# Masking one of six causal score tiles in VectorE's maximum instruction instead of by TensorE matmuls

## The reference, cut to what matters

```
causal_bias = where(i[None, :] <= i[:, None], 0.0, NEG)
for l in range(4):
    h = rmsnorm(x, n1[l])
    q, k, v = split(h @ Wqkv[l].T + bqkv[l], 3)
    q, k = apply_rope(q), apply_rope(k)
    s = einsum('bhqd,bhkd->bhqk', q, k) * scale + causal_bias
    x = x + (softmax(s) @ v merged over heads) @ Wo[l].T + bo[l]
    ... cross attention to the context, then a gated feed-forward block
```

## Time and profile before

| | us |
|---|---|
| median of 3 runs | 2112.79 (2111.06 to 2121.15) |
| time of the profiled execution | 2108.02 |
| its span, first to last instruction | 2106.3 |
| TensorE busy | 1821.6 (86%) |
| VectorE busy | 1414.7 (67%) |
| ScalarE busy | 1067.3 (51%) |
| GpSimd busy | 785.3 (37%) |

### The profile page before, as it was taken

One profiled execution on the slowest core, in us unless ns is written; L12 is line 12 of the kernel. 1 busy time (PEld: TensorE's weight loads), 2 busy tenths in 40 slices (PEclk: granted clock), 3 DMA queues, 4 the chain that ended last, 5 costly groups with the idle time before them and its releaser, 6 DMA issues. The chain is left out here.

```text
span 2106.3 us, 34605 instructions
## 1 busy us (share of the span) xinstructions
PE 1821.6 (86%) x12966; PEld 1123.3 (53%) x12971; DVE 1414.7 (67%) x3427; ACT 1067.3 (51%) x1523; POOL 785.3 (37%) x1131
## 2 busy tenths in 40 slices
PE   5978998584787898899899899999989999989978
PEld 4556665363454444565544464644555554456557
DVE  8667676552776877875577874577786466787475
ACT  2655655121453465564466566366656446656510
POOL 4423334403613554431455341255443154533130
PEclk9999998587787899999999999999999999999989
DMA  7443343121000000132000033000014000004200
GB/s 226 112 135 101 103 108 94 52 77 43 23 1 13 1 1 13 32 101 56 16 1 1 1 95 81 28 1 2 1 53 117 7 16 2 1 24 101 52 1 21
DMA packets 69995, 100.91 MB, mean 48 GB/s; under 512 B 17126, under 2 KB 35438, under 8 KB 69188
## 3 DMA queue, kind: packets, MB, share of 16 engines
q1 hardware_dynamic: 60612, 90.01, 14.9%
q0 software_dynamic: 9216, 8.69, 1.6%
HBM read 52.43 MB, written 12.38 MB: 31 GB/s over the span
## 5 line engine op out<-in xcount | busy, mean ns | idle before, releaser
L1778 DVE TENSOR_REDUCE maxima<-wide 128x2 f32<-128x512 f32 (+3 forms) x512 | 405.9, 818 | 133.7 <-PE wide L831 130.3
L2014 ACT ACTIVATE prob<-wide 128x768 f32<-128x768 f32 (+1 forms) x384 | 332.1, 881 | 146.0 <-PE wide L831 145.9
L1937 ACT ACTIVATE prob<-wide 77x1024 f32<-77x1024 f32 x256 | 257.8, 1017 | 91.9 <-PE wide L831 87.5
L831 PE MATMUL wide<-q_g 32*128 32x256 f32 (+3 forms) x2048 | 266.1, 390 | 38.2 <-ACT prob L2014 18.1
L2256 POOL TENSOR_SCALAR_AFFINE_SELECT prob<-prob 128x256 f32<-128x256 f32 (+1 forms) x384 | 184.8, 487 | 292.6 <-ACT prob L2014 291.0
L1454 DVE TENSOR_REDUCE maxima<-wide 128x8 f32<-128x616 f32 x256 | 202.8, 795 | 115.0 <-PE wide L831 109.4
L831 PEld LDWEIGHTS wide<-q_g 32*128 32x128 f32 x2048 | 138.4, 186 | 203.7 <-issue 99.8
L2078 POOL TENSOR_TENSOR rstd<-moments,cst 128x4 f32<-128x4 f32 x88 | 90.4, 1027 | 364.2 <-DVE moments L1342 171.5
L1858 ACT ACTIVATE q_g<-wide 128x1024 fp32r<-128x1024 f32 x128 | 131.1, 1024 | 185.0 <-PE wide L831 185.0
L831 PE MATMUL wide<-kx,q_g 128*128 128x312 f32 x512 | 180.7, 418 | 8.3 <-DVE maxima L1454 5.8
L2163 POOL DMA_DIRECT2D masked_k<-kx x224 | 121.3, 546 | 178.2 <-PE wide L831 177.0
(11 more groups left out here) (249 smaller groups left out, 3087.2 us busy)
## 6 DMA issues: line engine op xcount, KB each, us to landing
masked_q<-q_g SPq DMA_DIRECT2D x448, 64.0 KB
masked_q<-mask_l SPq DMA_DIRECT2D x84, 308.0 KB
masked_k<-kx POOLq DMA_DIRECT2D x224, 19.5 KB, 1.9
A<-in_w SPq DMA_DIRECT2D x2, 2048.0 KB, 11.9
unit_w<-in_unit_w SPq DMA_DIRECT2D x8, 448.0 KB, 3.8
ffn_w<-in_ffn_w SPq DMA_DIRECT2D x4, 768.0 KB, 4.7
slots_in<-v_third SPq DMA_DIRECT2D x1, 2560.0 KB, 12.4
prob<-slots_in SPq DMA_DIRECT2D x8, 320.0 KB, 3.3
```

What stands on the lines that cost most here:

```text
L831: return e.matmul(out, lhsT, rhs, start=start, stop=stop, is_transpose=turn)
L1778: e.tensor_reduce(top[:, t, h], v[:, :, at0:at0 + P * t + P], AX.X, ALU.max, negate=True).then_inc(*made("max", *([("free", tile)] if t == ...
L1937: e.activation(p[0:SC, :], s[0:SC, :], ACT.Exp, bias=0.0, scale=1.0).then_inc(*made("exp", pb, ("free", tile)))
L2014: e.activation(pv, sv, ACT.Exp, bias=0.0, scale=8 ** -0.5).then_inc(*made("exp", pb, ("free", tile)))
```

## The change

For the third tile (k = 2, `UNMASKED`) TensorE no longer adds the mask: its two matmuls with `causal_b` are left out, and the last score matmul of the tile is the one that VectorE waits for. In place of two `tensor_reduce` VectorE issues four `tensor_tensor_reduce`, one for each head and block: in0 is the scores in PSUM, in1 the mask as bf16 in SBUF, the sum is written back over the scores, and its largest value goes to `top`, one value per partition. To serve blocks of 128 and 384 columns alike, the constant is now a row of 384 zeros and the 128 columns of the mask, in bf16; a block of n columns takes the last n. It stands in `cst` as 256 words instead of 128. The maxima are no longer negated in any tile; instead the two rows of `k_tok` hold -1.0.

```
-for _n, _w in (("ident", P), ("causal", P), ...
+for _n, _w in (("ident", P), ("causal", S // 2), ...
+UNMASKED = 2
+        causal = const("causal").bitcast(BF)
 # TensorE, causal_max
-                        mm(s[:, at1:at1 + P * t + P], qk[r, 0, P * t:P * t + P], qk[r, 1, 0:P * t + P],
-                           start=t == blocks[0], stop=False)
+                        i_mm = mm(s[:, at1:at1 + P * t + P], qk[r, 0, P * t:P * t + P], qk[r, 1, 0:P * t + P],
+                                  start=t == blocks[0], stop=k == UNMASKED and t == blocks[-1])
-                for c in range(2):
+                for c in range(2 if k != UNMASKED else 0):
 # VectorE, begin
-            e.tensor_copy(causal_b[:, :], const("causal")).then_inc(*made("begin"))
+            e.tensor_copy(causal_b[:, :], causal[:, S - P:S]).then_inc(*made("begin"))
 # VectorE, causal_max
                 for t in blocks:
-                    e.tensor_reduce(top[:, t, h], v[:, :, at0:at0 + P * t + P], AX.X, ALU.max, negate=True).then_inc(
-                        *made("max", *([("free", tile)] if t == blocks[-1] else [])))
-                    at0 += P * t + P
+                    n, ends = P * t + P, [("free", tile)] if t == blocks[-1] else []
+                    if k == UNMASKED:
+                        for c, i in enumerate(heads_in):
+                            part = s[:, S * c + at0:S * c + at0 + n]
+                            e.tensor_tensor_reduce(part, part, causal[:, S - n:S], 1.0, NEG, ALU.add, ALU.max,
+                                                   top[:, t, i:i + 1]).then_inc(*made("max", *(ends if c == 1 else [])))
+                    else:
+                        e.tensor_reduce(top[:, t, h], v[:, :, at0:at0 + n], AX.X, ALU.max).then_inc(*made("max", *ends))
+                    at0 += n
 # GpSimd, clear
-                e.memset(k_tok[:, :, :, MROW:MROW + 2], 1.0).then_inc(*made("clear"))
+                e.memset(k_tok[:, :, :, MROW:MROW + 2], -1.0).then_inc(*made("clear"))
 # constants
-    put("causal", np.where(r[None, :] > r[:, None], NEG, 0.0))
+    late = np.concatenate([np.zeros((P, S - P)), np.where(r[None, :] > r[:, None], NEG, 0.0)], 1).astype(np.float32)
+    put("causal", (late.view(np.uint32) >> 16).astype(np.uint16).view(np.float32))
```

More of the change, by code:

```diff
@@ L37 @@
 _at = 0
-for _n, _w in (("ident", P), ("causal", P), ("cumul", P), ("cos", NI * 8), ("sin", NI * 8),
+for _n, _w in (("ident", P), ("causal", S // 2), ("cumul", P), ("cos", NI * 8), ("sin", NI * 8),
                ("kscale8", 1), ("kscale4", 1), ("pick", 2), ("position", NI), ("iota", SC), ("rev", E8), ("minus_half", NI),
@@ L156 @@
     tensor_reduce = tensor_copy = memset = reciprocal = bn_stats = bn_aggr = affine_select = dma_start = anything
-    indirect_dma_start = anything
+    indirect_dma_start = tensor_tensor_reduce = anything
 def interleaved(items):
```

## The result

The changed kernel took 2121.42 us (median of 11 runs) beside 2111.06 for the kernel before (11 runs, same chip): ratio 1.0058, 95% interval 1.004 to 1.0077. The medians are 10.4 us apart and the ratio makes 12 us, where 12 had been forecast. The profiled execution has a span of 2116.7 us, against 2106.3.

The account below looks back on a forecast made before the run. TensorE's order was taken to set the pace. VectorE's later return of the third tile summed to 13.8 us, less some 2 for short waits: 12 us on the 2112.79 median made 2124.8 us, range 2109 to 2150.

Parts of the forecast that it names:

- TensorE's saving is worth nearly nothing: Ahead of the fourth score tile: 20 us of removed matmuls only lengthen the wait for ScalarE, from 0.28 to 0.60 us.
- Rival 4: Ahead of the fourth tile: the wait shrinks in 48 groups by 0.32 us each, 15 us, giving 2097; chance 0.04.
- D = 1.80 us: VectorE's work on the third tile: four combined instructions take 1.80 us against 1.29 for the two reductions.
- rival 1: VectorE's third tile: the value beside the output is free, work 1.50 us, about +1 us, giving 2114; chance 0.28.
- four times 0.074 for the value beside the output: VectorE's third tile: each of the four instructions pays 0.074 us for its one value per partition, on top of 1.50.
- The starts: VectorE begins the third tile 0.32 us earlier where it was idle, not where it comes straight from other work.
- the turn waits for VectorE in nearly every group: TensorE's qk_turn for the next group waits for VectorE to return the third tile, by 0.12 to 0.42 us.
- the 25 groups: Commonest kind of head group: the next group's turn comes 0.19 us later in each, 4.8 us in all.
- the 8: Groups where VectorE comes straight from the key and query cut, without earlier start: 0.42 us each, 3.4 us.
- the 4: Groups where the turn already waits 0.50 us for VectorE: the end moves 0.19 us each, 0.8 us in all.
- The 11 groups: Second kind of head group: the turn at 1455.96 instead of 1455.84, 0.12 us each, 1.3 us in all.
- rival 3: VectorE's third tile: writing into PSUM in place halves the rate, work 2.88 us, about +70 us, 2183; chance 0.09.

Follow-up runs that it names:

- e1: Changed kernel, but TensorE also keeps its two mask matmuls on the third tile, so it is masked twice: 2123.43 us, ratio 1.0056 to before.
- e2: Changed kernel with no mask at all on the third tile, VectorE using plain reductions: 2103.93 us, ratio 0.9965 to before.
- e12: Changed kernel with the filler of e9 plus 20 matmuls of 256 zero columns inside the idle time in layer 0: 2107.02 us, ratio 1.000.
- e10: Kernel before (TensorE masks all six tiles, only the maxima's sign as in the changed kernel) with the filler of e9: 2095.13 us, ratio 0.9962.
- e3: Changed kernel with two matmuls of 256 zero columns added to one logits tile of every group: 2112.71 us, ratio 1.001 to before.
- e9: Changed kernel with matmuls of 384 zero columns in four groups: five in the second of layers 1 to 3, three in the sixth of layer 0; ratio 1.0026.
- e11: Changed kernel with no mask in any of the six maximum tiles, VectorE using plain reductions: 2088.27 us, ratio 0.993 to before.

## Why the prediction was right, and where it was not

The time came out 3.4 us below the forecast, and for a sum of which only about half was the right term. The kernel before, measured again, came out 1.7 us below the median that the forecast started from.

- *TensorE's saving is worth nearly nothing.* Right, and the row is the wait ahead of the fourth tile: 1.07, 1.08, 1.08 and 1.08 us after the exponential in before, changed, e1 and e2. Forecast for it was a wait of 0.60 us, measured 0.75, because the two matmuls held TensorE for 0.47 us and not for 0.32; with the wait behind them this cost nothing. Rival 4 (faster) fell on this row. e2 shows the limit of "nearly nothing": 0.07 us in the common groups, but 0.3 in fourteen others, some 5 us of the 20.
- *D = 1.80 us.* Mis-sized: 1.64 (median of the groups 1.635), halfway between it and rival 1's 1.50. The step that was mis-sized is "four times 0.074 for the value beside the output". The instructions follow one another every 0.49, 0.51 and 0.25 us, and three of the four accumulator reads run beside the next main instruction. What counts is one read of 0.14 us at the end: 1.50 + 0.14 = 1.64. The Trainium skill, "VectorE: DVE Perf Modes", section "Two Vector instructions with no wait between them", is borne out in that such an operation is two instructions; the price that I had put on the second one was my own, from the trains of bn_aggr in the earlier trace rows, and its place was wrong.
- *The starts.* Right: VectorE begins 0.32 us earlier relative to the exponential (0.09 us after it instead of 0.41), and where it comes straight from other work, as in the earlier trace rows, it doesn't. The counterpart of that row in the changed kernel:

```profile
1481.90 0.73 DVE L1274 TENSOR_SCALAR hid<-rope_b 128x512 int32<-128x512 int32 x1 [0.81 <-POOL rope_b L2240]
...
1482.56 0.55 DVE L1788 CUSTOM_DVE_ANT_0 wide<-wide,cst 128x384 f32<-128x384 f32 x1
...
1484.24 0.66 PE L836 MATMUL wide<-cst,hid 128*128 128x128 f32 x4
```

  The turn starts 1.68 us after the custom instruction, 1.43 in the earlier trace rows; these 8 groups lost 0.30 us each. The sign that the turn waits for VectorE in nearly every group, came in about half: in 35 of the 64 the turn's weight load waits for it, by 0.16 us in the common groups and 0.36 in those of the earlier trace rows; in groups such as the one shown after the result it does not.
- *The terms by kinds.* With D = 1.64 each forecast falls by 0.16 us: 0.03 (measured 0.02) for the 25 groups, 0.26 (0.30) for the 8, 0.03 (0.02) for the 4, and 0.35 for the second to fourth of layer 0. There the two filled kernels (e12 and e10), whose time at the low clock in these groups is the same, differ by 0.30, 0.17 and 0.35. Two terms were wrong for their own sake. The 11 groups lost 0.07 where -0.04 would follow (VectorE starts only 0.27 us earlier in them; the rest is not accounted for), and the first groups of the layers nothing instead of 0.15. In the latter the third tile's reductions start 1.19 us after the group's first reduction instead of 1.48, so 0.29 us earlier and not the 0.20 of idleness in the earlier trace rows that I had allowed. The last groups of the layers lost 0.23 each, 0.9 together, forecast 1.0. Layer 0 lost 1.3 us and layer 1 1.1 between the filled kernels; with layers 2 and 3 taken as layer 1 and the last groups added, that makes 5.5 us for the mechanism for which 12 had been forecast. The quiet groups give 5.6 and 6.1 with the last groups added.
- *The rival that was missing.* No rival had the clock in it. I had read 1.00 in the two windows of the earlier trace rows and argued from steady stretches, where it is 1.00 after the change as well. The profile of before held the sign: 79 us at the lower level between 640 and 1890 us, most of them in the first groups of layers, where TensorE waits for other engines. At one place, the sixth group of layer 0, the changed kernel lost 3.5 us by it in both profiles and the kernel before nothing. In the second groups of layers 1 to 3 the clock fell in all six cases of the changed kernel, but in five of six of the kernel before. This filled up the sum to the measured time, which was luck and no merit of the forecast. The ratios of the fillers do not prove it: beside 1.0058 and 1.0044 of the changed kernel, e3 and e9 have 1.001 and 1.0026 with intervals that overlap the 1.0044, and e12's 1.000 holds the scatter named above. What shows it is the groups.
- *The first DMA and the casts* brought nothing that shows: the first self-attention group of the changed kernel begins at 650.66 us, 6.4 us earlier than in before (657.05). That is scatter of the stage ahead; in other profiles of this study it begins at 652.46 (e12) and 640.60 (e9). For the same reason one pair of spans is not the measure of a change of 0.5%.

Left open: why the clock falls in the sixth group of layer 0 in the changed kernel and not in the kernel before, though TensorE is idle there for 2.45 and 2.44 us. It fell 1.5 to 2.4 us into the idle time in all six profiles without TensorE's mask on the third tile in which that time was left (changed twice, e2, e3, e9, e11), and with the second or the sixth tile left to VectorE; it did not fall with the fifth, nor in the four with all six masks on TensorE (before twice, e1, e10). That TensorE had done less in the microseconds ahead is a guess; no run isolates it. The slower groups two and three of layer 0 (+0.65 and +1.46 us with a stretch of 27 us at the lower level, 14 in before) are not explained either. The third took 15.7 us in e1, which only adds VectorE's work, and in e2, which only takes TensorE's away, and 14.47 in e12, which has the whole change.

## What to carry to other kernels

- Ask of removed work on the busiest engine what comes next on it. Where the next thing is a wait that another engine ends, the saving is mostly idle time; here 52 us of TensorE's work bought 14.6 us.
- A buffer that comes back later costs only what it exceeds the next limit by: write the two ends beside each other for each kind of group, and look for the groups in which the engine has no idle time to start earlier in.
- Look at the granted clock in the places where TensorE waits, not only in the steady stretch. Find by narrow windows in which idle time it falls, for the longest is not always the one. Matmuls of zeros in that time won 3.7 us in one group here; a filler behind it did nothing there.
- A few groups at the low clock move this kernel by several us from one execution to the next. Two profiles of the same kernel differed by 4.5 us over the 60 groups (before, twice), so a change of half a per cent is read from the groups that the clock leaves alone.

## What the runs showed of the hardware

- A tensor_tensor_reduce on VectorE, PSUM in place with a bf16 mask from SBUF, takes 580 ns for 384 elements and 330 for 128, or one each 0.50 and 0.25 us in a train: the rate of the plain reduction (1.05 ns in the earlier trace rows). Writing into PSUM beside reading it costs nothing, so rival 3 (half the rate) has fallen.
- Its accumulator read (140 ns) starts together with the next main instruction, and shows only behind the last one.
- The granted clock fell to 0.50 after TensorE had been idle for 2.45 us in one kernel and stayed at 1.00 after 2.44 in the other. In the second group of layer 2 of the changed kernel it was down before the wait of 1.45 us began, and in the second groups of the kernel before, with waits of 0.53 and 0.98 us, it fell in five of six cases. Such a fall cost up to 2.96 us in the second groups and 3.5 in the sixth of layer 0.
- 20 matmuls of 256 zero columns in that idle time (2.36 us) kept the clock at 1.00 and shortened the group from 14.2 to 10.54 us.
